# Second batch's attention scores in two halves of two row strips, the first half ahead of the first batch's values; second batch's value products in the first two FFN banks

## The reference

```python
x = x + xattn(layernorm(x), ctx, ctx, ...)
x = x + ffn(layernorm(x), ...)

# xattn, for each of 8 heads of width 32
log_fg = log_sigmoid(f_pre); lf = cumsum(log_fg)          # gates: 15*tanh(pre/15)
log_d  = lf[t+1] - lf[s+1] + i_pre[s], -inf where s > t
m      = max(log_d over s);  d_mat = exp(log_d - m)
s_mat  = (q @ k.T) / sqrt(32) * d_mat
h      = s_mat @ v / (max(|sum(s_mat)|, exp(-m)) + 5e-5)
h      = h * rsqrt(mean(h*h) + 1e-6) * (1 + outnorm_w)

# ffn, hidden width 1024, ternary weights
h = silu(x @ w1.T * s1) * (x @ w2.T * s2)
h = gelu(h @ h1.T * sh1);  h = gelu(h @ h2.T * sh2)
return h @ w3.T * s3
```

## Time and profile before

| | us |
|---|---|
| median of 3 runs | 753.38 |
| lowest, highest | 753.29, 753.94 |
| profiled execution, its own time | 753.1 |
| profiled execution, span of the trace | 751.3 |

### The profile page before, as it was taken

How to read it: one execution, slowest core, us unless ns; L and a number is a source line. 1 busy time by engine, 2 the same in 40 slices (tenths; PEclk the granted TensorE clock), 3 DMA queues, 4 the chain that set the end, 5 groups by cost and what they waited for, 6 DMA issues and landing times.

```text
span 751.3 us, 15005 instructions
## 1 busy us (share of the span) xinstructions
PE 743.0 (99%) x6112; PEld 607.5 (81%) x6112; DVE 550.4 (73%) x1270; ACT 373.9 (50%) x568; POOL 23.8 (3%) x52
## 2 busy tenths in 40 slices
PE   8999999999999999999999999999999999999998
PEld 4778888888888888888888888888888888888886
DVE  6788678586976969688695868858696774755764
ACT  3585527463456626456354653646345562445332
POOL 3400000000000000000000000000000000000000
PEclk9999999999999999999999999999999999999999
DMA  9294224303052021611225021530206100230761
GB/s 333 82 416 165 58 63 133 149 13 102 9 197 85 29 87 26 222 41 30 86 81 206 1 62 60 153 128 29 88 7 205 50 1 3 87 138 21 257 217 40
DMA packets 23335, 78.09 MB, mean 104 GB/s; under 512 B 6385, under 2 KB 8033, under 8 KB 20449
## 3 DMA queue, kind: packets, MB, share of 16 engines
q1 hardware_dynamic: 21680, 64.80, 25.9%
q0 software_dynamic: 1296, 11.53, 3.9%
q10 hardware_dynamic: 288, 0.79, 0.3%
HBM read 63.96 MB, written 13.14 MB: 103 GB/s over the span
## 4 chain that ended last, share of the span: by engine, by line
PE 94%; DVE 1%; ACT 0%; issue 0%
PE ps_f L1657 32%; PE ps_f L1658 31%; PE ps_f L1622 8%; PE ps_f L1623 8%; PE ps_f L1694 4%; PE ps_f L1695 4%; PE ps_a L1562 2%; PE ps_a L1545 2%; PE ps_a L1404 1%; PE ps_a L1595 1%; PE ps_a L1517 1%; PE ps_a L1554 0%; PE ps_f L1632 0%; DVE stats L1135 0%; DVE z L1122 0%; DVE rms L1113 0%
## 5 line engine op out<-in xcount | busy, mean ns | idle before, releaser
L1657 PE MATMUL ps_f<-h_hi,wgt 128*128 128x512 f32 x1024 | 402.1, 393 | 0.0
L1658 PE MATMUL ps_f<-h_lo,wgt 128*128 128x512 f32 x1024 | 398.8, 389 | 0.0
L1657 PEld LDWEIGHTS ps_f<-h_hi,wgt 128*128 128x128 f32 x1024 | 192.2, 188 | 41.6 <-ACT work L810 1.2
L1658 PEld LDWEIGHTS ps_f<-h_lo,wgt 128*128 128x128 f32 x1024 | 192.3, 188 | 39.0
L810 ACT ACTIVATE work<-ps_f,scl 128x512 f32<-128x512 f32 x128 | 87.6, 685 | 211.2 <-PE ps_f L1658 208.5
L1241 DVE TENSOR_TENSOR h_lo<-work,h_hi 128x512 fp32r<-128x512 f32 x128 | 85.6, 688 | 72.7 <-ACT h_hi L813 72.0
L1622 PE MATMUL ps_f<-h_hi,wgt 128*128 128x512 f32 x252 | 99.1, 393 | 0.0
L1623 PE MATMUL ps_f<-h_lo,wgt 128*128 128x512 f32 x252 | 98.2, 390 | 0.0
L1232 DVE SCALAR_TENSOR_TENSOR work<-ps_f,scl,work 128x512 f32<-128x512 f32 x64 | 48.0, 750 | 48.1 <-PE ps_f L1623 47.2
L813 ACT ACTIVATE h_hi<-work 128x512 fp32r<-128x512 f32 x128 | 81.0, 633 | 4.1
L797 ACT ACTIVATE work<-ps_f,scl 128x512 f32<-128x512 f32 x64 | 44.1, 689 | 77.8 <-PE ps_f L1623 77.1
(11 more groups left out here) (208 smaller groups left out, 616.3 us busy)
## 6 DMA issues: line engine op xcount, KB each, us to landing
decay<-m_rows SPq DMA_DIRECT2D x14, 1024.0 KB, 7.7
decay<-w_cols SPq DMA_DIRECT2D x22, 512.0 KB, 4.6
z<-moment_rows SPq DMA_DIRECT2D x13, 512.0 KB, 4.0
wgt<-w_cols POOLq DMA_DIRECT2D x5, 1024.0 KB, 11.6
v_aug<-ctx_tok SPq DMA_DIRECT2D x8, 528.0 KB, 5.1
wgt<-w_cols POOLq DMA_DIRECT2D x2, 2048.0 KB, 13.6
z_kept<-num SPq DMA_DIRECT2D x8, 512.0 KB, 8.1
x_kept<-xs SPq DMA_DIRECT2D x8, 512.0 KB, 3.2
```

The lines of the kernel that those rows point to most:

```text
L1657: pe.matmul(ps_f[:, bank], w, moving(h_hi[layer][:, k], as_is), start=(k == 0), stop=False)
L1658: last = pe.matmul(ps_f[:, bank], w, moving(h_lo[layer][:, k], as_is), start=False, stop=(k == KH - 1))
```

## The change

`scores(0, 1)` becomes two calls of a new `first_scores(half)`, each of the eight products of two row groups (two row strips). The first half (row groups 0 and 1, banks 0 and 1 of `ps_f`) stands ahead of `first_values(0, 0)` and waits for the decays of banks 0 and 1. The second half stands where `scores(0, 1)` stood. `weigh_scores(0, 1)` becomes two calls of `weigh_second_half`, two instructions each, in the order 0, 1, 2, 3; the first pair stands ahead of `take_state(0)`. `value_out(0, 1, t)` becomes bank t of `ps_f`, and `first_values(1, part)` goes through the row groups in order. `first_values(0, 1)` uses the form with four strips of 32 columns like the others.

```diff
+            def weigh_second_half(half):
+                if half:
+                    dve.wait_ge(s_qk, W)
+                    dve.wait_ge(s_exp, EXP_STEPS)
+                else:
+                    dve.wait_ge(s_qk_half, 1)
+                    dve.wait_ge(s_exp_third, 1)
+                for r in range(half * ROWGRP // 2, (half + 1) * ROWGRP // 2):
+                    s = score_tiles(1)[:, :, r]
+                    dve.scalar_tensor_tensor(s, score_out(0, 1, r).rearrange("p (c n) -> p c n", c=CH), SCORE_SCALE, s, ALU.mult, ALU.mult)\
+                       .then_inc(s_smat, 1)
...
                 if bank % 2:
                     last.then_inc(s_exp, 1)
+                elif bank == 2:
+                    last.then_inc(s_exp_third, 1)
...
-                return (ps_f if b else ps_a)[:, 2 + t, 0:HEADS * DV]
+                return (ps_f[:, t] if b else ps_a[:, 2 + t])[:, 0:HEADS * DV]
...
             weigh_scores(0, 0)
+            weigh_second_half(0)
             take_state(0)
-            weigh_scores(0, 1)
+            weigh_second_half(1)
             take_far(0)
...
+            def first_scores(half):
+                pe.wait_ge(s_exp, EXP_STEPS if half else EXP_STEPS - 1)
+                for t in range(TILES):
+                    for c in range(CH):
+                        for r in range(half * ROWGRP // 2, (half + 1) * ROWGRP // 2):
+                            d = slice(r * DH, (r + 1) * DH)
+                            col = (c * TILES + t) * P
+                            at = slice((TILES + t) * P, (TILES + t + 1) * P)
+                            last = pe.matmul(score_out(0, 1, r)[:, col:col + P], ctxT(0)[d, c, at], zT(0)[d, c, at], start=True, stop=True)
+                last.then_inc(s_qk if half else s_qk_half, 1)
...
-                for r in FIRST_WEIGHED[2 * part:2 * part + 2]:
+                weighed = range(ROWGRP) if b else FIRST_WEIGHED
+                for r in weighed[2 * part:2 * part + 2]:
                     for h in (r, r + ROWGRP):
                         for t in range(TILES):
-                            if (b, part) == (0, 1):
-                                for n in range(W):
-                                    strip = slice(n * P // W, (n + 1) * P // W)
-                                    last = pe.matmul(value_out(0, b, t)[strip, h * DV:(h + 1) * DV], decay_of(b, h, t)[:, strip],
-                                                     v_aug[:, b * TILES + t, h, :], start=True, stop=True)
-                            else:
-                                last = values_of_head(0, b, h, t)
+                            last = values_of_head(0, b, h, t)
...
             pe.wait_ge(s_v, 16)
+            first_scores(0)
             first_values(0, 0)
             make_state(0)
-            scores(0, 1)
+            first_scores(1)
             first_values(0, 1)
```

More of the change, by code:

```diff
@@ L225, in build @@
         s_exp = sem("s_exp")
+        s_exp_third = sem("s_exp_third")
+        s_qk_half = sem("s_qk_half")
         s_qk = sem("s_qk")
@@ L1534, in scores @@
                     reuse(pe, s_num, j)
-                elif first(j):
-                    pe.wait_ge(s_exp, EXP_STEPS)
                 else:
```

## The result

The changed kernel takes 754.09 us (median of 13 runs, 753.04 to 755.40) against 753.14 us for the kernel before (13 runs, 752.65 to 753.94). The ratio is 1.0016, with a 95% interval of 1.0008 to 1.0023: slower, and within the 0.2% taken as no change. The forecast was 753.7 with a range of 752.8 to 754.6. As a difference, 0.28 was forecast and 0.95 came. What was forecast for the prologue came in size almost as said, but most of the difference lies elsewhere.

What follows compares the result with a forecast made beforehand. TensorE was taken to set the pace from the first FFN product, VectorE's chain the prologue before it. TensorE's +1.10, -0.35, -0.23 made it 0.52 later, `take_far` and the sums +0.28: 753.38 to 753.7 us, range 752.8 to 754.6.

Steps and rivals of the forecast that it cites:

- something not listed: Anywhere in the kernel: an effect outside the named cases, on either side, no size given; chance 0.04.
- Halves of the scores: Batch 1's scores on TensorE: each half over two strips lasts 1.10 us like the whole, so 2.20 instead of 1.10.
- The first rival: Score halves on TensorE: records 0.028 apart whatever the strips, a half takes 0.67 us; -0.59, 752.8 us; chance 0.15.
- the second: Score halves on TensorE: loads lie bare, 1.99 us each instead of 1.10; +2.06, 755.4 us; chance 0.06.
- Values in 32 columns: Batch 0's values, second part, on TensorE: 0.71 us in the 32-column form instead of 1.06, saving 0.35.
- `take_far`: VectorE in the prologue: waits about 0.5 us for the state's reading and starts at 31.96 instead of 31.68, +0.28.
- The sign of being wrong, a start before 31.6: VectorE in the prologue: the prediction is wrong if `take_far` starts before 31.6 us.
- The second sum: VectorE, prologue: at 33.22 us after `take_far` and the first sum; batch 1's values allow 33.21, just in time.
- From the sums on: Prologue behind the two sums: the chain to the first FFN product keeps its parts, only shifted by +0.28 us.
- the 0.1 that was given as a sign of being wrong: Prologue after 33.4 us: the prediction is wrong if a gap there changes by more than 0.1 us.
- No transfer is issued from a new place: Transfers of the program: none is issued from a new place; no cost was booked for them.
- the four cases: Whole kernel: likeliest, with nothing moving included, 0.75; halves at half cost 0.15; bare loads 0.06; anything unlisted 0.04.

Runs made afterwards that it cites:

- after_lo7: The changed kernel with VectorE's `norm_in_place`, which waits for the transfer of x_t, moved behind the last `h_lo` of the first hidden layer; 752.91 us, ratio 1.0003 to before.
- after_pad192: The changed kernel with 192 unawaited semaphore increments on TensorE in the first pair, 48 after each of four groups; 776.70 us, ratio 1.0317 to before.
- after_even192: The changed kernel with 192 unawaited semaphore increments spread behind products of the first pair's two hidden layers on TensorE; 754.10 us, ratio 1.0016 to before.
- rs_first: The changed kernel with `read_state(0)` ahead of `first_values(0, 1)`; 753.89 us, ratio 1.0011 to before.
- before_32: The kernel before with only `first_values(0, 1)` put in strips of 32 columns, 64 more TensorE instructions; 753.66 us, ratio 1.0008 to before.
- again: The changed kernel, unedited, run again; 753.92 us, ratio 1.0012 to before.
- after_64: The changed kernel with `first_values(0, 1)` put back to 64-wide strips, as many TensorE instructions as before; 753.79 us, ratio 1.0010 to before.
- before_lo7: The kernel before with VectorE's `norm_in_place` moved behind the last `h_lo` of the first hidden layer; 752.92 us, ratio 1.0000 to before.
- before_even64: The kernel before with 64 unawaited semaphore increments, one after each second product of the first pair's first hidden layer; 753.82 us, ratio 1.0009 to before.

## Why the prediction was right where it was, and what it missed

The measured time lies in the range, and the mechanism in the prologue is the one forecast. That the whole lies there is luck in part: the prologue gives 0.31 of the 0.95 us, and for the rest the prediction had no term, only the 0.04 that it left for something not listed.

- **Halves of the scores: right.** 1.10 from start to start was said; 26.40 to 27.49 is 1.09. The first rival (0.67) needed records at one pace whatever the strips, and the second (1.99) bare loads. The rule of the Trainium skill, "TensorE: Matmul & The Clock Gate", section Part 3 (What overlaps and what doesn't), that a load overlaps products only of other row groups would have had the second. The trace disagrees here too: L1573's loads are 0.187 long, and with two strips each strip starts a record every 0.11.
- **Values in 32 columns: right.** 0.71 said, 29.59 to 30.28 is 0.69.
- **`take_far`: right in kind, half in size.** It was to be 0.28 later with a new wait of about 0.5. The wait is 0.49, the delay 0.14. The sign of being wrong, a start before 31.6, was given on the clock of the profile before; 31.48 is 31.82 there, counted from the last spread. The terms off are the state's group, counted at its length of 0.46 where the next group starts 0.39 after it, the hand-over, 0.03 instead of 0.07, and 0.03 in small parts.
- **The second sum: the forecast holds without the gap.** Said 33.22 less 26.54, 6.68; in after_lo7, after_pad192 and after_even192 it is 6.64. It comes there by the other of the two paths that the prediction had as level: from `take_far`, VectorE alone would be at 6.55 (5.28, the first sum 0.80 later, 0.47 more), and TensorE's values of batch 1 hold it until 6.64. In the first two profiles of the changed kernel it is 6.81 and 6.84, since batch 1's values take 1.50 there. The gap has no named releaser. Among the kernels with the 32-wide form it is there, 0.1 to 0.3 us, where TensorE's last fetch before it took 12.9 to 16.6% of 16 engines over half a microsecond, that is 1.0 to 1.3 us (rs_first, before_32, changed, again), and not where it took 10.9 to 12.1% (after_pad192, after_lo7, after_even192). With the 64-wide form, 64 instructions fewer in the stretch, there is none even at 17.5% (after_64). The longest gap (before_32, 0.27) goes with 14.1% and a shorter one (again, 0.19) with 16.6%, so the share doesn't give the size. That would be the dry instruction stream again; it wasn't tested by itself.
- **From the sums on: nearly right.** 12.01 us to the first FFN product instead of 12.11. L1154 (L1171 after), the first of the denominators, is 0.22 long and was 0.34; why, no row shows. The gaps of VectorE behind it are as before within 0.01, but gaps of the other engines changed by more than the 0.1 that was given as a sign of being wrong (ScalarE's 0.67 to 0.42 before L668 and 0.76 to 0.92 before L755, TensorE's none to 0.30 before L1498). The way to the first FFN product got no longer by them. The total of 0.31 against 0.28 said is therefore partly luck: 0.14 + 0.27 - 0.10. Without the gap the prologue costs 0.15 to 0.17.
- **"No transfer is issued from a new place": the step that failed.** It is true of the transfers in the program, and I had looked only at those. The 64 instructions more that the 32-wide form puts on TensorE (the term that was booked as a saving of 0.35) move each later fetch of its instructions, by up to 2 us at x_t. The page before listed 49 fetches of 16 KB in its DMA queues, and the program's own `s_even` increments, one or two for each block of the FFN, for which nobody waits, may have hinted at their weight. None of the four cases had it. Its size, in the profiles with 64 instructions more and nothing in the way, is 0.4 to 1.8 us, and it depends on how late x_t lands in that execution, because VectorE has some 0.8 us to spare at that place: in the fourth pair it was 1.45 us late behind the transfer and TensorE only 0.67.

The Trainium skill, "Runtime: NRT & Kernel Launch", section Instruction fetch mechanics, says that instructions are fetched in blocks of 256 by the sequencer's own queue and that crossing a block is "mostly hidden". The fetches agree in number (49 for 12,224 recorded instructions, 249 each). That they are hidden holds in most places for the engine that fetches; for the transfer beside it the pairs above disagree.

The kernel before stays the best of all that ran, with before_lo7 and after_lo7 level with it. With the wait for x_t moved, the change costs what the prologue costs (0.15 in the profiles), and that is below what the runs resolve.

What stays open: the gap in batch 1's values, TensorE's stop in after_even192, and why a fetch that falls into x_t takes up to twice as long and delays it by up to 1.5 us, since only the queue's share is to be seen and not which engine serves what.

## What to carry to other kernels

Splitting a packed group of small products into groups of fewer row strips cost as much here as doubling it; split along something that keeps all strips busy. After moving a wait off one engine, add up the other engine's whole work to the next hand-over: here 0.24 us of slack, 0.23 of idle time and 0.35 saved stood against 1.10 added. And in a kernel that runs within a fraction of a microsecond of its slack, compare the landing times of transfers in code that was not touched, and where the instruction fetches fall, before a difference is put down to the edit.

## What the hardware showed that I had not expected

- 64 instructions more on TensorE, doing nothing, made a 512 KB transfer land later in each of its six issues, 0.3 to 1.5 us (the median of x_t went from 3.7 to 4.9 us). They cost 1.8 us in one profile, and 1.0009 (0.9999 to 1.0018) in the medians.
- A semaphore increment on TensorE takes some 0.09 us when 48 stand in a row, and the granted clock was 0.58 in the four microseconds behind them. One behind each second product of 0.23 us cost nothing (before_even64).
- Records of products over 64 columns start every 0.029 us, those over 32 columns every 0.010 in twice the number: 0.61 us for the work that took 1.06. The wide form saves instructions and not time.
